# Norm and router arithmetic moved from GpSimd to VectorE, a bias moved into a matmul, FFN rounding moved into PSUM evictions, and new engine orders, in a two-layer fused kernel

## The chip, the cores and the metric

One Trainium2 chip, one of its cores. The metric is the device time of one execution in microseconds (us). The five engines are TensorE (PE; its weight loads are shown apart as PEld), VectorE (DVE), ScalarE (ACT), GpSimd (POOL) and SyncE (SP, which here only issues DMAs). Each has its own program and its own sequence of instructions; they meet through semaphores.

## The reference

Sixteen batches of 128 tokens by 128 features run through four residual stages:

```python
x = x + tanh(g_xattn[0]) * xattn0(ctx, ctx, layernorm(x))   # stage a: 16 heads, softmax over the HEADS
x = x + tanh(g_ffn[0])   * moe(layernorm(x))                # stage m: 8 experts, top 2, silu(x w0) * (x w1) -> wo
x = x + tanh(g_xattn[1]) * xattn1(layernorm(x), ctx)        # stage f: cat[c, c2q, c*c2q, c*q2c] @ W_l.T + b_l
x = x + tanh(g_ffn[1])   * bitffn(layernorm(x))             # stage g: 128 -> 512 gate/up -> 128

layernorm(x) = (x - mean(x)) / sqrt(var(x) + 1e-5)
moe:    w = softmax(top2(x @ gate)); sum over the 2 chosen experts of w * expert(x)
bitffn: each activation is scaled by 127/max|x| of its row and rounded to whole numbers
        ahead of each matmul; weights are rounded to -1, 0, 1 times their mean size
```

## The kernel before

The batches go through in eight pairs (256 tokens each). All four stages of a pair run on the one core, and neighbouring pairs overlap: while pair p is in the experts, pair p+1 is in attention and pair p-1 in the stages f and g. Weights stay in SBUF; SP loads them at the start. Matmuls of stages a and m are split into a high and a low part (`_hi`, `_lo`, three matmuls per product, `ps_z<-m_xhi,w_hi`, `m_xhi,w_lo`, `m_xlo,w_hi`).

**The order of the work.** Every engine's program is a list of steps, and two tables, `WHEN` (a step of each pair) and `ONCE` (a step of the start, and the spare matmuls `pe.warm_*`), give each step a number per pair; `order(engine)` sorts an engine's steps by these numbers. The tables thus set the order on each engine alone; waits between engines are semaphores.

**Stage a.** K and Q are projected, split into three bf16 parts (`qk_parts`), stored by SP to `rows_dram` and fetched as `k_rows` and `q_rows`. Four units per pair then go through `head_max` (DVE), `shifted` (DVE), `attn<-shifted` (ACT, the exponential), `tree` (POOL, four adds that sum over the heads), `head_inv` (DVE) and `attn<-attn,head_inv` (POOL). Then the weighted values, the output projection and x1.

**A layernorm** (a, m, f and g: four a pair, 32 in all) is `BN_STATS` and `BN_AGGR` on DVE (`*_mv`), four tiny instructions of 128x2 on POOL in `rstd` (add eps, negate the mean, raise to the power -1/2, multiply), and two ACT instructions that apply scale and bias.

**Stage m.** Sixteen up tiles: PE writes `ps_z`, ACT makes `m_tanh`, DVE `m_u`, and DVE or POOL `m_h` (POOL has seven of the sixteen). Eight `down` products go to `ps_d`; the first two experts' are added to `y` by ACT and POOL, the other six by DVE (`y<-ps_d,weights,y`). The router takes the difference of the top two logits (`tdiff`, DVE), its exponential (`texp`, ACT), five tiny POOL instructions for the two probabilities (`pool.top_probs`), and on DVE four instructions and a sum that make `weights`.

**Stage f** ends with four products into `late_bank` (`pe.f_z`) and, on DVE, x3 = th * product + `y_res`, where POOL has made `y_res` = `y` + bias (`pool.y_res`).

**Stage g** rounds by adding the constant `ROUND` (1.5 * 2^23) in f32 and taking it off again. The first activation: `g_r` (ACT, adds it), `g_q` (DVE, takes it off, to bf16), a PE transpose, `g_qt` (ACT copies out of PSUM). The second: `g_pr` (ACT, adds it), `g_pq` (ACT, takes it off, to bf16), four PE transposes for a batch, `g_pt` (ACT copies out of PSUM), the down product.

Each pair writes one `y`, so POOL's first add of a pair waits until the pair before has read it. `spare` issues PE matmuls on an identity (`ps_f<-ident_bf`) whose result nobody reads.

Of the kernel before, what the change touches and what calls it, by code (L numbers as in the profile page):

```python
# [13 lines left out]
P = 128  # L14
# [33 lines left out]
    "sp.load_a": (12, 1501, 2546, 3638, 7464, 12475, 17304, 20931),  # L48
    "sp.store_parts": (
# [6 lines left out]
    ),  # L56
    "sp.fetch_rows": (
        (1960, 3826, 7126, 11165, 15185, 19034, 23535, 27447),
        (2176, 3979, 7280, 10827, 14847, 18694, 23197, 27600),
    ),  # L60
    "sp.load_res": (2646, 5144, 9928, 12576, 16625, 22383, 25012, 28949),
    "sp.load_f": (2697, 11318, 15338, 19216, 24905, 27785, 31537, 34931),
    "sp.store": (16288, 20577, 24859, 28736, 32637, 36238, 38259, 39516),
    "pool.a_rstd": (467, 2292, 3414, 4828, 11299, 16757, 20361, 24484),
    "pool.ct_lo": (399, 2108, 2915, 8603, 12228, 13500, 20286, 21743),
    "pool.part3": (
        (1032, 2533, 6643, 10304, 14257, 18449, 22272, 26895),
        (1821, 3535, 7016, 10717, 14736, 18386, 23086, 27337),
    ),
    "pool.head_sum": (  # L70
# [4 lines left out]
    ),  # L75
    "pool.head_norm": (
# [14 lines left out]
    ),  # L91
    "pool.top_probs": (6705, 10149, 14319, 18585, 22334, 26625, 30788, 33972),
    "pool.y_res": (10367, 13574, 18312, 21817, 25821, 29981, 33448, 36784),
    "pool.f_rstd": (9408, 13378, 17534, 21621, 25895, 30055, 33522, 36662),
    "pool.f_prod": (11082, 15324, 19402, 23525, 27788, 31830, 34983, 37677),
    "pool.g_rstd": (12106, 15779, 20090, 24057, 28227, 32433, 35617, 38044),
    "pool.out": (16206, 20488, 24778, 28655, 32555, 36140, 38177, 0),
# [275 lines left out]
}  # L373

ONCE = {
    "sp.w_moe": 358,
    "sp.w_out": 113,
    "sp.w_fin": 1005,
    "sp.w_ffn": 853,
# [1435 lines left out]
```

## Time and profile before

| | |
|---|---|
| time, median of 3 runs | 398.3 us (397.81 to 398.43) |
| span of the profiled execution | 397.3 us |
| busy PE, PEld | 324.9, 284.0 us (82%, 71%) |
| busy DVE, POOL, ACT | 313.1, 299.1, 256.4 us (79%, 75%, 65%) |
| first `head_max` of pair 0, 1, 2, 3, 4, 7 | 28.2, 47.4, 81.4, 119.9, 159.4, 281.9 us |

The profile is of one execution; its span lies 1.0 us under the median. Busy times of the engines overlap, so none of them is the time. The first `head_max` of a pair marks where that pair's attention begins: from pair 3 to pair 7 the four pairs between are 162.0 us, 40.5 us each. The stretch before 28.2 us loads and splits weights; behind 320 us the last pair is alone.

### The profile page before, as it was taken

To read this page: it belongs to the slowest core of one execution; us is meant where nothing else is said; L and a number is where in the kernel's file an instruction comes from. 1 tells how busy PE (TensorE), PEld (TensorE's weight loads), DVE (VectorE), ACT (ScalarE), POOL (GpSimd) and SP (SyncE) were. 2 spreads that over 40 slices of the span, in tenths; PEclk is the share of its full clock that TensorE was granted. 3 is DMA by queue.
4 is the path that set the end of the run, shared out by engine and by line. 5 is a ranking of instruction groups with operands and counts; after the bars stand their busy time and mean duration, and the time that the engine had idled before them with its cause. 6 is when DMAs were issued, how large, how long until landed. Compare 5 with 4: busy or idle time off the path is not lost.

```text
span 397.3 us, 10407 instructions
## 1 busy us (share of the span) xinstructions
PE 324.9 (82%) x3326; PEld 284.0 (71%) x3326; DVE 313.1 (79%) x913; ACT 256.4 (65%) x726; POOL 299.1 (75%) x459
## 2 busy tenths in 40 slices
PE   1365589898999789979998899879978997996875
PEld 1255469787898679867986698669957896994742
DVE  2679877598869997999799979995989678778434
ACT  4335254536846797779667885777658855875754
POOL 4378989799898989898999799988778873443010
PEclk9999767999999999999999999998999999999585
DMA  5967210300341114012401221204100000000000
GB/s 161 289 192 210 81 36 21 116 17 16 88 115 34 29 41 128 19 56 63 108 15 47 68 87 29 61 6 131 33 16 1 28 15 2 2 29 14 2 13 13
DMA packets 34454, 24.17 MB, mean 61 GB/s; under 512 B 3617, under 2 KB 32097, under 8 KB 34401
## 3 DMA queue, kind: packets, MB, share of 16 engines
q1 hardware_dynamic: 33680, 23.32, 19.7%
q8 instruction: 27, 0.44, 0.5%
q10 hardware_dynamic: 720, 0.20, 0.2%
q14 instruction: 27, 0.21, 0.2%
HBM read 16.16 MB, written 7.34 MB: 59 GB/s over the span
## 4 chain that ended last, share of the span: by engine, by line
PE 37%; POOL 25%; DVE 13%; issue 10%; ACT 7%; DMA 4%; SPq 3%; POOLq 0%; DVEq 0%; ACTq 0%
POOL tree L939 9%; PE ps_d L1448 8%; POOL attn L945 8%; PE ps_z L1188 4%; PE ps_a L1196 3%; PE ps_z L1189 3%; PE ps_z L1190 3%; POOL m_h L876 2%; DVE head_max L1584 2%; DMA wf_raw<-in_wd 2%; DVE m_u L1623 1%; DMA k_rows<-rows_dram 1%; DVE y L1655 1%; PE ps_sc L1234 1%; DVE shifted L1590 1%
## 5 line engine op out<-in xcount | busy, mean ns | idle before, releaser
L1188 PE MATMUL ps_z<-m_xhi,w_hi 128*128 128x256 f32 x240 | 76.9, 320 | 12.7 <-DVE m_h L1631 6.1
L945 POOL TENSOR_TENSOR attn<-attn,head_inv 128x1024 f32<-128x1024 f32 x32 | 75.8, 2371 | 0.2 <-DVE head_inv L1606 0.2
L1448 PE MATMUL ps_d<-wdn,m_h 128*128 128x128 f32 x512 | 71.4, 283 | 4.7 <-DVE m_h L1631 2.1
L1448 PEld LDWEIGHTS ps_d<-wdn,m_h 128*128 128x128 f32 x512 | 63.1, 194 | 8.5 <-issue 4.1
L1189 PE MATMUL ps_z<-m_xhi,w_lo 128*128 128x256 f32 x240 | 68.8, 287 | 0.0
L1190 PE MATMUL ps_z<-m_xlo,w_hi 128*128 128x256 f32 x240 | 68.6, 286 | 0.0
L1623 DVE SCALAR_TENSOR_TENSOR m_u<-m_tanh,ps_z 128x256 f32<-128x256 f32 x120 | 49.0, 411 | 17.6 <-ACT m_tanh L1033 16.7
L1033 ACT ACTIVATE m_tanh<-ps_z 128x256 f32<-128x256 f32 x120 | 45.9, 384 | 26.0 <-PE ps_z L1190 25.6
L1188 PEld LDWEIGHTS ps_z<-m_xhi,w_hi 128*128 128x128 f32 x240 | 46.7, 195 | 19.3 <-issue 6.1
L876 POOL TENSOR_TENSOR m_h<-m_u,m_z 128x256 f32<-128x256 f32 x56 | 41.1, 734 | 17.2 <-DVE m_u L1623 17.2
L939 POOL TENSOR_TENSOR tree<-tree 128x256 f32<-128x256 f32 (+2 forms) x90 | 46.4, 515 | 7.1
L1189 PEld LDWEIGHTS ps_z<-m_xhi,w_lo 128*128 128x128 f32 x240 | 46.9, 196 | 0.0
L1190 PEld LDWEIGHTS ps_z<-m_xlo,w_hi 128*128 128x128 f32 x240 | 46.7, 195 | 0.0
L939 POOL TENSOR_TENSOR tree<-attn 128x512 f32<-128x512 f32 x30 | 38.3, 1277 | 6.5 <-ACT attn L1046 6.3
L1584 DVE TENSOR_REDUCE head_max<-ps_sc 128x64 f32<-128x1024 f32 x32 | 38.9, 1215 | 4.5 <-PE ps_sc L1234 4.2
L1046 ACT ACTIVATE attn<-shifted 128x1024 f32<-128x1024 f32 x32 | 33.7, 1055 | 10.1 <-DVE shifted L1590 10.1
L1590 DVE TENSOR_TENSOR shifted<-ps_sc,head_max 128x1024 f32<-128x1024 f32 x32 | 38.8, 1213 | 0.3
L1655 DVE SCALAR_TENSOR_TENSOR y<-ps_d,weights,y 128x128 f32<-128x128 f32 x96 | 28.8, 342 | 4.5 <-PE ps_d L1448 3.1
L1631 DVE TENSOR_TENSOR m_h<-m_u,ps_z 128x256 f32<-128x256 f32 x67 | 27.6, 414 | 5.8 <-PE ps_d L1448 5.1
L1031 ACT ACTIVATE m_z<-ps_z 128x256 f32<-128x256 f32 x53 | 20.2, 381 | 14.6 <-PE ps_z L1190 13.8
L1196 PE MATMUL ps_a<-attn,v_diag 128*32 128x128 f32 x512 | 20.4, 290 | 3.7 <-POOL attn L945 3.3
L1234 PE MATMUL ps_sc<-q_rows,k_rows 48*128 48x64 bf16 x512 | 13.7, 196 | 7.7 <-DVE shifted L1590 5.6
(311 smaller groups left out, 852.0 us busy)
## 6 DMA issues: line engine op xcount, KB each, us to landing
rows_dram<-qk_parts SPq DMA_DIRECT2D x16, 192.0 KB, 2.2
k_rows<-rows_dram SPq DMA_DIRECT2D x16, 192.0 KB
q_rows<-rows_dram SPq DMA_DIRECT2D x16, 192.0 KB
w_raw<-in_w SPq DMA_DIRECT2D x2, 1024.0 KB, 7.9
rows_dram<-qk_parts SPq DMA_DIRECT2D x16, 128.0 KB, 2.0
x_in<-in_x SPq DMA_DIRECT2D x8, 128.0 KB, 2.4
ct_in<-in_ctx_t SPq DMA_DIRECT2D x8, 128.0 KB, 2.4
rows_dram<-qk_parts SPq DMA_DIRECT2D x16, 64.0 KB, 1.7
```

The costliest lines, as they stand in the source:

```text
L876: pool.tensor_tensor(m_h[:, k % 4], m_u[:, k % 4], m_z1[:, n % 3], ALU.mult).then_inc(s_mhp, 1)
L939: pool.tensor_tensor(dst, src[:, 0:n, :], src[:, n:2 * n, :], ALU.add).then_inc(s_tree, 1)
L945: pool.tensor_tensor(e, e, head_inv[:, u % 2].unsqueeze(1).to_broadcast([P, HEADS, HALF]), ALU.mult).then_inc(s_attn, 1)
L1033: act.activation(m_tanh[:, k % 2], tile_bank(p, k)[:, 0:TOK], ACT.Tanh, scale=0.5).then_inc(s_mt, 1)
L1046: act.activation(attn[:, b, :, k0:k0 + HALF], shifted[:, u % 2], ACT.Exp).then_inc(s_exp, 1)
L1188: pe.matmul(dst, hi_w, hi_x, start=start, stop=False)
L1189: pe.matmul(dst, lo_w, hi_x, start=False, stop=False)
L1190: return pe.matmul(dst, hi_w, lo_x, start=False, stop=True)
L1448: last = pe.matmul(ps_d[:, b * P:(b + 1) * P], m_h[:, m % 4, b * P:(b + 1) * P], wdn[:, m], start=(k == 0), stop=(k == TPE - 1))
L1584: dve.tensor_reduce(head_max[:, u % 2], sc.rearrange("p h k -> p k h"), AX.X, ALU.max).then_inc(s_hmax, 1)
L1590: dve.tensor_tensor(shifted[:, u % 2], sc, head_max[:, u % 2].unsqueeze(1).to_broadcast([P, HEADS, HALF]), ALU.subtract).then_inc(s_shift, 1)
L1623: dve.scalar_tensor_tensor(m_u[:, k % 4], m_tanh[:, k % 2], 1.0, z[:, 0:TOK], ALU.add, ALU.mult).then_inc(s_mu, 1)
```

## The change

- `rstd` on POOL keeps only the power. The eps add (`add_eps`) and the product with the negated mean (`minus_mean_rstd`) become two DVE steps for each norm, each with a place of its own in DVE's order. ACT's norm waits for the second.
- The router's five POOL instructions become four on DVE (`dve.top_probs`, with a reciprocal in place of the power). The four that made `w_first` and `w_second` become two over both batches and both places (`top_eq`, `top_w`).
- `pool.y_res` goes. The bias of stage f is a third plane of `bias_parts` and is added by PE, one more matmul of `first_products` for each batch; x3 reads `y` itself. `y` has two buffers.
- Stage g: PE transposes the f32 values `g_r` and `g_pr`, and `ROUND` is taken off as the result leaves PSUM: `g_qt` (now on DVE) and `g_pt` (ACT). `g_q` (DVE), `g_qt` on ACT and `g_pq` (ACT) go.
- The third-stage bias is loaded as 96x128 with the stage a biases, not as 128x128. Three constants of the start go.
- All numbers of `WHEN` and `ONCE` are new.

```diff
-    "sp.load_a": (12, 1501, 2546, 3638, 7464, 12475, 17304, 20931),
+    "sp.load_a": (1, 658, 1926, 4484, 8345, 12225, 15475, 18558),
...
-            def rstd(p, s_mv, s_rs, mv, rs):
-
-                pool.wait_ge(s_mv, p.count(2, 2))
-                pool.tensor_tensor(rs[:, 0], mv[:, :, 1], eps_col[:], ALU.add).then_inc(s_rs, 1)
-                pool.tensor_tensor(rs[:, 1], mv[:, :, 0], minus_ones[:], ALU.mult).then_inc(s_rs, 1)
-                pool.wait_ge(s_rs, p.count(4, 1))
-                pool.tensor_tensor(rs[:, 2], rs[:, 0], minus_half[:], ALU.pow).then_inc(s_rs, 1)
-                pool.wait_ge(s_rs, p.count(4, 3))
-                pool.tensor_tensor(rs[:, 3], rs[:, 2], rs[:, 1], ALU.mult).then_inc(s_rs, 1)
+            def rstd(p, s_rs, s_norm, rs):
+
+                pool.wait_ge(s_rs, p.count(3, 1))
+                wait(pool, s_norm, p.before().count(2, 2))
+                pool.tensor_tensor(rs[:, 0], rs[:, 2], minus_half[:], ALU.pow).then_inc(s_rs, 1)
...
+            def add_eps(p, mv, rs, s_mv, s_rs):
+
+                dve.wait_ge(s_mv, p.count(2, 2))
+                dve.tensor_scalar(rs[:, 2], mv[:, :, 1], EPS, None, ALU.add).then_inc(s_rs, 1)
+
+            def minus_mean_rstd(p, mv, rs, s_rs):
+
+                dve.wait_ge(s_rs, p.count(3, 2))
+                dve.scalar_tensor_tensor(rs[:, 1], mv[:, :, 0], -1.0, rs[:, 0], ALU.mult, ALU.mult).then_inc(s_rs, 1)
...
-                if p := due(now, "pool.top_probs"):
-
-                    pool.wait_ge(s_texp, p.count(1, 1))
...
+                if p := due(now, "dve.top_probs", 0):
+
+                    dve.wait_ge(s_texp, p.count(1, 1))
+                    dve.tensor_scalar(tsum[:], texp[:], 1.0, None, ALU.add).then_inc(s_tp, 1)
+                if p := due(now, "dve.top_probs", 1):
+                    dve.wait_ge(s_tp, p.count(4, 1))
+                    dve.reciprocal(tinv[:], tsum[:]).then_inc(s_tp, 1)
+                if p := due(now, "dve.top_probs", 2):
+                    dve.wait_ge(s_tp, p.count(4, 2))
...
+                    dve.tensor_scalar(tprob[:, :, 0:1], tinv[:], th_half[:, 0:1], None, ALU.mult).then_inc(s_tp, 1)
+                    dve.scalar_tensor_tensor(tprob[:, :, 1:2], texp[:], th_half[:, 0:1], tinv[:], ALU.mult,
+                                             ALU.mult).then_inc(s_tp, 1)
...
-                    for b in range(2):
-                        for k, dst in enumerate((w_first, w_second)):
-                            dve.tensor_scalar(dst[:, b], expert_no[:], top_nof[:, b, k:k + 1],
-                                              tprob[:, b, k:k + 1], ALU.is_equal, ALU.mult).then_inc(s_w12, 1)
+                    dve.wait_ge(s_tp, p.count(4, 4))
+                    dve.wait_ge(s_teq, p.count(1, 1))
+                    dve.tensor_tensor(top_w[:], top_eq[:], tprob[:].unsqueeze(3).to_broadcast([P, 2, 2, EXPERTS]),
+                                      ALU.mult).then_inc(s_w12, 1)
...
-                if p := due(now, "pool.y_res"):
...
-                    pool.tensor_tensor(y_res[:], y[:], bl_all[:].unsqueeze(1).to_broadcast([P, 2, P]),
-                                       ALU.add).then_inc(s_fyb, 1)
...
+            def first_products(p, b):
+
+                s = slice(b * P, (b + 1) * P)
+                pe.matmul(late_bank(p, b)[:, s], ones_bf[:], bias_parts[:, 2], start=True, stop=False)
+                pe.matmul(late_bank(p, b)[:, s], f_ct[:, s], wl[:, 0], start=False, stop=False)
...
-                    if p := due(now, "act.g_pq", b):
-
-                        act.wait_ge(s_gpr, p.count(2, b + 1))
-                        wait(act, s_gpt, p.before().count(2, 2))
-                        act.activation(g_pq[:, b], g_pr[:, b], ACT.Copy, bias=-ROUND).then_inc(s_gpq, 1)
...
-                        act.activation(g_pt[:, b], batch_bank(p, b)[:, 0:TOK].bitcast(BF16), ACT.Copy).then_inc(s_gpts, 1)
+                        act.activation(g_pt[:, b], batch_bank(p, b)[:], ACT.Copy, bias=-ROUND).then_inc(s_gpts, 1)
...
-                            pe.transpose(batch_bank(p, b)[:, k * HALF:(k + 1) * HALF].bitcast(BF16),
-                                                g_pq[:, b, k * P:(k + 1) * P], ident_bf[:])
+                            pe.transpose(batch_bank(p, b)[:, k * P:(k + 1) * P],
+                                                g_pr[:, b, k * P:(k + 1) * P], ident[:])
...
-                if p := due(now, "dve.g_q"):
-                    wait(dve, s_gqt, p.before().count(1, 1))
...
+                if p := due(now, "dve.g_qt"):
+                    wait(dve, s_gu, p.before().count(4, 4))
...
+                        dve.tensor_scalar(g_qt[:, cols(g)], batch_bank(p, g[0])[:, cols(g)], ROUND, 127.0, ALU.subtract,
+                                          ALU.min).then_inc(s_gqs, 1)
```

Where the tables put things is read from the order of the built programs. First SP at the start. `w_raw` are the expert weights w0 and w1 (1 MB each), `wf_raw` the three FFN weights, `gains`, `bias_raw` and `wo_t` belong to stage a's output, `wcq` and `bsum` to stage f; before, from the first load of `x_in` and `ct_in` on:

```order
L756 DMA gains<-in_g_xattn 128x2
...
L760 DMA wo_t<-in_wo 128x128
L750 DMA w_raw<-in_w 128x8x256
...
L770 DMA wf_raw<-in_wd 128x4x128
L763 DMA wcq<-in_w_cq 128x1
...
L766 DMA bl_all<-in_bl 128x128
L791 DMA rows_dram<-qk_parts 128x3x256 [waits s_k1]
```

and after:

```order
L755 DMA w_raw<-in_w 128x8x256
...
L774 DMA wf_raw<-in_wd 128x4x128
L761 DMA gains<-in_g_xattn 128x2
...
L765 DMA wo_t<-in_wo 128x128
L783 DMA x_in<-in_x 128x2x128 [waits s_axn]
L785 DMA ct_in<-in_ctx_t 128x2x128 [waits s_ctlo]
L795 DMA rows_dram<-qk_parts 128x3x256 [waits s_k1]
```

The bulk loads now lead, the seven small loads of `wcq`, `bsum` and `bl_all` no longer stand ahead of the first store of `qk_parts` (six of them follow the fetches of `q_rows`), and the next pair's two loads do.

Second, POOL in a middle pair, at a norm. Before, that of stage g, with `m_h` ahead of it and `attn` behind:

```order
L876 TENSOR_TENSOR m_h<-m_u,m_z 128x256
L843 TENSOR_TENSOR g_rs<-g_mv,eps_col 128x2
L844 TENSOR_TENSOR g_rs<-g_mv,minus_ones 128x2
L846 TENSOR_TENSOR g_rs<-g_rs,minus_half 128x2
L848 TENSOR_TENSOR g_rs<-g_rs 128x2
L945 TENSOR_TENSOR attn<-attn,head_inv 128x16x64
```

and after, those of stages m and f:

```order
L873 TENSOR_TENSOR m_h<-m_u,m_z 128x256
L845 TENSOR_TENSOR m_rs<-m_rs,minus_half 128x2
L920 TENSOR_TENSOR attn<-attn,head_inv 128x16x64
L892 TENSOR_TENSOR o_sb<-o_raw,x 128x256
L845 TENSOR_TENSOR f_rs<-f_rs,minus_half 128x2
```

A norm is now one POOL instruction of 128x2 where there were four. What DVE holds between the two tiny instructions of stage m's norm, L1465 (eps) and L1470 (the product), in a middle pair after the change:

```order
L1465 TENSOR_SCALAR m_rs<-m_mv 128x2
L1615 SCALAR_TENSOR_TENSOR m_u<-m_tanh,ps_z 128x256
L1752 RECIPROCAL g_sc<-g_amc 128x2
L1753 SCALAR_TENSOR_TENSOR g_sc<-g_amc,cg 128x2
L1615 SCALAR_TENSOR_TENSOR m_u<-m_tanh,ps_z 128x256
L1623 TENSOR_TENSOR m_h<-m_u,ps_z 128x256 x2
L1647 SCALAR_TENSOR_TENSOR y<-ps_d,weights,y 128x128 x2
L1470 SCALAR_TENSOR_TENSOR m_rs<-m_mv,m_rs 128x2
L1576 TENSOR_REDUCE head_max<-ps_sc 128x64
```

Eight of DVE's instructions lie between the two, and the next unit's `head_max` stands right behind the one that waits for POOL.

Third, PE between the value projection of pair 1 (`ps_a<-ct_hi,wqkv_hi`) and pair 0's gate, before:

```order
L1188 MATMUL ps_a<-ct_hi,wqkv_hi 128x256
L1189 MATMUL ps_a<-ct_hi,wqkv_lo 128x256
L1190 MATMUL ps_a<-ct_lo,wqkv_hi 128x256
L1243 MATMUL ps_d<-ident,m_xn 128x128 x2
L1213 MATMUL ps_f<-ident_bf 128x128 x8
L1234 MATMUL ps_sc<-q_rows,k_rows 128x64 x16
```

and after:

```order
L1152 MATMUL ps_a<-ct_hi,wqkv_hi 128x256
L1153 MATMUL ps_a<-ct_hi,wqkv_lo 128x256
L1154 MATMUL ps_a<-ct_lo,wqkv_hi 128x256
L1184 MATMUL ps_f<-ident_bf 128x128 x32
L1233 MATMUL ps_a<-ident,a_xn 128x128 x2
L1214 MATMUL ps_d<-ident,m_xn 128x128 x2
L1184 MATMUL ps_f<-ident_bf 128x128 x12
L1205 MATMUL ps_sc<-q_rows,k_rows 128x64 x16
```

Where eight spare matmuls (`ps_f`) stood, there are 44.

## Rows read from the trace of the kernel before

**Rows 1.** Windows of the span; us, then busy time (instructions) by engine, clock, DMA.

```profile
28.15:119.90 91.75, 75.50 (x899) 67.78 (x899) 73.39 (x173) 47.16 (x125) 83.06 (x112) 0.91 0.27 81
119.90:281.90 162.00, 143.68 (x1540) 127.47 (x1538) 142.69 (x431) 120.72 (x351) 144.65 (x222) 0.99 0.20 58
320.00:397.30 77.30, 62.59 (x475) 51.59 (x473) 50.22 (x180) 49.47 (x146) 24.48 (x50) 0.87 0.04 12
```

**Rows 2.** POOL timeline at 158 us: start, length, engine, line, operation, tiles.

```profile
158.44 0.20 POOL L843 TENSOR_TENSOR g_rs<-g_mv,eps_col 128x2 f32<-128x2 f32 x1
...
158.74 0.70 POOL L846 TENSOR_TENSOR g_rs<-g_rs,minus_half 128x2 f32<-128x2 f32 x1
...
159.66 2.38 POOL L945 TENSOR_TENSOR attn<-attn,head_inv 128x1024 f32<-128x1024 f32 x1
```

**Rows 3.** POOL timeline at 144 us, the router.

```profile
144.66 0.21 POOL L885 TENSOR_TENSOR tsum<-texp,ones 128x2 f32<-128x2 f32 x1
...
146.16 0.73 POOL L876 TENSOR_TENSOR m_h<-m_u,m_z 128x256 f32<-128x256 f32 x1
```

**Rows 4.** Instructions by line, POOL, 28 to 320 us: count, busy, mean ns, idle before.

```profile
L889 POOL TENSOR_TENSOR tsum<-tsum,minus_one 128x2 f32<-128x2 f32 x7 | 4.9, 700 | 0.5
L846 POOL TENSOR_TENSOR m_rs<-m_rs,minus_half 128x2 f32<-128x2 f32 x7 | 4.9, 699 | 0.0
...
L912 POOL TENSOR_TENSOR y_res<-y,bl_all 128x256 f32<-128x256 f32 x6 | 4.4, 731 | 0.0
L846 POOL TENSOR_TENSOR f_rs<-f_rs,minus_half 128x2 f32<-128x2 f32 x6 | 4.2, 700 | 0.0
L846 POOL TENSOR_TENSOR a_rs<-a_rs,minus_half 128x2 f32<-128x2 f32 x6 | 4.2, 694 | 0.0
L846 POOL TENSOR_TENSOR g_rs<-g_rs,minus_half 128x2 f32<-128x2 f32 x5 | 3.5, 701 | 0.0
```

**Rows 5.** Waits of POOL, 28 to 320 us: who, for whom, us, times, longest.

```profile
POOL tree L939 <- ACT attn L1046: 6.3, 8, 1.3
...
POOL qk_parts L869 <- ACT qk_parts L1022: 3.6, 2, 2.2
POOL tsum L885 <- ACT texp L1079: 1.6, 3, 0.9
```

**Rows 6.** Instructions by line, ACT: count, busy us, mean ns, idle before.

```profile
L1172 ACT ACTIVATE g_pq<-g_pr 128x512 bf16<-128x512 f32 x16 | 10.0, 627 | 0.0
```

**Rows 7.** SP timeline, the first 24 us (issues, not landings).

```profile
4.13 0.43 SPq L750 DMA_DIRECT2D w_raw<-in_w  x1
...
5.23 3.38 SPq L754 DMA_DIRECT2D gate_raw<-in_gate  x1
...
10.08 1.20 SPq L763 DMA_DIRECT2D wcq<-in_w_cq  x1
...
14.17 1.50 SPq L791 DMA_DIRECT2D rows_dram<-qk_parts  x3
```

**Rows 8.** DVE timeline at the start.

```profile
16.23 1.75 DVE L1542 TENSOR_REDUCE wabs<-wf_raw 128x3 f32<-128x1536 f32 x1 [3.22 <-DMA wf_raw<-in_wd]
...
28.15 1.23 DVE L1584 TENSOR_REDUCE head_max<-ps_sc 128x64 f32<-128x1024 f32 x1 [0.52 <-PE ps_sc L1234]
```

**Rows 9.** Window with the clock at half, 55.1 to 65.3 us.

```profile
55.10:65.30 10.20, 9.67 (x60) 8.80 (x61) 8.86 (x21) 5.29 (x12) 9.73 (x12) 0.50 0.11 33
```

**Rows 10.** Chain that ended last, 390 to 395 us: start, length, what.

```profile
392.29 0.62 ACT g_pq L1172
```

**Rows 11.** Two DVE lines with two SBUF inputs: ns min/median/max.

```profile
L1669 DVE TENSOR_TENSOR weights<-w_first,w_second x8: 163/174/260, 71.8 to 343.0; 128x16 f32<-128x16 f32 x8
...
L1642 DVE TENSOR_TENSOR tdiff<-top x8: 144/330/657, 64.5 to 339.1; 128x2 f32<-128x2 f32 x8
```

**Rows 12.** DVE timeline at 146 us, and the same line in the page, part 5.

```profile
146.24 0.74 DVE L1623 SCALAR_TENSOR_TENSOR m_u<-m_tanh,ps_z 128x256 f32<-128x256 f32 x2
...
L1623 DVE SCALAR_TENSOR_TENSOR m_u<-m_tanh,ps_z 128x256 f32<-128x256 f32 x120 | 49.0, 411 | 17.6 <-ACT m_tanh L1033 16.7
```

More of the change, by code:

```diff
@@ L92 @@
[L92 to L97, printed above, removed]
[7 rows of a table added]
+    ),
+    "pool.f_prod": (9223, 12965, 16563, 20126, 23964, 27864, 30805, 33218),
@@ L373 @@
+    "dve.top_probs": (
[3 rows of a table added]
+    ),
+    "dve.top_eq": (5196, 8762, 12397, 15981, 19303, 23401, 26825, 30376),
+    "dve.g_qt": (10808, 14746, 18452, 21713, 25584, 28985, 31976, 33985),
 }
 ONCE = {
[L376 to L379, printed above, removed]
-    "sp.w_late": 2804,
-    "act.qkv_hi": (717, 371, 697),
-    "act.w_hi": (1899, 1476, 4321, 1804),
-    "act.gate_hi": 2328,
-    "act.th": 851,
-    "pool.w_lo": (1588, 2685),
-    "pe.w_total": 1735,
-    "dve.qkv_scale": (382, 1305),
@@ new lines @@
+    "act.th": 1095,
+    "pool.w_lo": (1429, 1837),
+    "pe.w_total": 1181,
+    "dve.qkv_scale": (599, 781),
+    "dve.qkv_lo": (705, 685, 1521),
+    "dve.w_lo": (4625, 5783),
+    "dve.gate_lo": 4282,
+    "dve.w_small": 4576,
+    "dve.w_abs": 1003,
+    "dve.w_scale": 1582,
+    "dve.w_round": (1637, 1703, 2044),
+    "dve.w_clip": (3123, 3730),
+    "dve.bias_parts": 1169,
+    "act.wo_scale": 3230,
+    "pe.warm_f": (32220, 32242, 32509, 32531, 32552, 32797, 32818, 32840, 32862, 32994, 33016, 33217, 34064, 34086),
@@ L602, in build @@
         f_w4 = sb("f_w4", [P, 2, P])
-        y_res = sb("y_res", [P, 2, P])
         x3s = sb("x3", [P, 2, 2, P])
@@ L614, in build @@
         g_r = sb("g_r", [P, 2, P])
-        g_q = sb("g_q", [P, 2, P], BF16)
         g_qt = sb("g_qt", [P, TOK], BF16)
@@ L1077, in _ @@
                     act.wait_ge(s_tdf, p.count(1, 1))
-                    wait(act, s_tp, p.before().count(5, 5))
+                    wait(act, s_tp, p.before().count(4, 4))
                     act.activation(texp[:], tdiff[:], ACT.Exp).then_inc(s_texp, 1)
@@ L1140, in _ @@
                     act.wait_ge(s_gsc, p.count(3, 3))
-                    wait(act, s_gq, p.before().count(1, 1))
+                    wait(act, s_gqt, p.before().count(1, 1))
                     for b in range(2):
@@ L1147, in _ @@
                     act.activation(g_sc[:, :, 1], g_amc[:], ACT.Identity, scale=cg[:, 0:1]).then_inc(s_gsz, 1)
-                if p := due(now, "act.g_qt"):
-                    wait(act, s_gu, p.before().count(4, 4))
-                    for g in groups(p):
-                        act.wait_ge(s_gqt, p.count(1, 1) + g[0])
-                        act.activation(g_qt[:, cols(g)], batch_bank(p, g[0])[:, g[0] * HALF:(g[-1] + 1) * HALF].bitcast(BF16),
-                                       ACT.Copy).then_inc(s_gqs, 1)
                 for u in range(4):
@@ L1163, in _ @@
                         act.wait_ge(s_gps, p.count(4, 2 * b + 2))
-                        wait(act, s_gpq, p.before().count(2, b + 1))
+                        wait(act, s_gpt, p.before().count(2, b + 1))
                         act.activation(g_pr[:, b], g_p[:, b], ACT.Identity, scale=g_ps[:, b, 0:1],
@@ L1486, in stats @@
             def stats(p, x, st, mv, s_st, s_mv, s_rs):
-                wait(dve, s_rs, p.before().count(4, 4))
+                wait(dve, s_rs, p.before().count(3, 3))
                 for b in range(2):
@@ L1643, in _ @@
                     dve.wait_ge(s_topi, p.count(2, 2))
-                    wait(dve, s_w12, p.before().count(4, 4))
+                    wait(dve, s_teq, p.before().count(1, 1))
                     dve.tensor_copy(top_nof[:], top_no[:]).then_inc(s_tnof, 1)
@@ L1668, in _ @@
                     wait(dve, s_y, p.before().count(2 * DVE_SUMS, 2 * DVE_SUMS))
-                    dve.tensor_tensor(weights[:], w_first[:], w_second[:], ALU.add).then_inc(s_w, 1)
+                    dve.tensor_tensor(weights[:], top_w[:, :, 0], top_w[:, :, 1], ALU.add).then_inc(s_w, 1)
                 if p := due(now, "dve.a_xlo"):
```

399 lines of the change are left out of this document (197 added, 202 removed), and 271 rows, old and new, of the table WHEN.

## The prediction

> **What bounds the kernel now.** I read the windows first, because shares over the whole span mix four different stretches. From the first `head_max` to pair 3's, 91.75 us, POOL is busy for 83.06 us, more than PE (75.50) or DVE (73.39). In the middle, four pairs in 162.00 us, three engines stand close together: POOL 144.65, PE 143.68, DVE 142.69, each about 89%. Behind 320 us the last pair is alone and POOL has 24.48 of 77.30 us: there a chain of latencies sets the end [rows 1]. So up to 320 us I take POOL as the engine on which the others wait, by a narrow margin in the middle.
>
> Then POOL's timeline, to see what it does between the large instructions. A norm begins at 158.44, its power starts at 158.74 and the next large instruction at 159.66: 1.22 us for four instructions that work on two numbers a row, with the power .77 (158.74 to 159.51) of it [rows 2]. The five router instructions hold POOL from 144.66 to 146.16, 1.50 us [rows 3]. Last, POOL's waits between 28 and 320 us. The largest that ACT causes are 6.3 us ahead of `tree`, 3.6 ahead of `qk_parts`, 1.6 ahead of the router's first instruction [rows 5]. So POOL is not wholly a wall: some of its idle time is ACT being late.
>
> At the start POOL is no limit: SP is. The store of `qk_parts` is issued at 14.17, behind a row of small loads from 10.08 on and behind `gate_raw`, whose issue took 3.38 us [rows 7]. DVE waits 3.22 us for `wf_raw` and then spends 1.75 on its absolute sums; the first `head_max` comes at 28.15 [rows 8].
>
> **The change part by part, against the span of 397.3 us.**
>
> *Tiny work off POOL.* Between 28 and 320 us the power has 24 rows (m 7, f 6, a 6, g 5), the router 7, `y_res` 6 at .73 us [rows 4]. A norm keeps its power: 1.22 − .77 = .45 saved. 24 × .45 = 10.8; 7 × 1.5 = 10.5; 6 × .73 = 4.4; together 25.7 us. Where POOL is the engine waited for, the end moves by all of it: **−25.7**. That is at once the largest term and the most doubtful, since in the middle the other engines have only 1 to 2 us less work than POOL. The lower bound of the gain is what the next engine allows, below under the rivals.
>
> *What DVE gets.* A pair has 14 new tiny instructions (8 for norms, 4 for probabilities, 2 for weights). The nearest row is the sum of the weights, 163 ns at least and 174 in the median [rows 11]: at most 14 × .174 = 2.4 us a pair, if each cost its whole row. They don't quite: two `m_u` in a row fill .74 us where their line has a mean of 411 ns [rows 12], so rows overlap at their ends. And four instructions for the router's weights and `g_q` go. I take the net at nothing on the path, because DVE's own idle time covers it (162.00 − 142.69 = 19.3 us over four pairs, 4.8 a pair) [rows 1]; the other end is the whole 2.4 a pair.
>
> *What PE gets.* Four f32 transposes in place of bf16 ones for a batch, and one more product of 128 columns for each. PE stands idle 18 us of the 162 [rows 1]; nothing on the path, and in the last pair a few tenths, which I take against the saved rows there.
>
> *ACT.* `g_pq` goes: 16 of 627 ns, 10.0 us [rows 6], and the copy for `g_qt` goes to DVE. ACT is no bound anywhere, but POOL waits for it. The wait ahead of the router's POOL work (1.6) goes with that work; of the 9.9 us ahead of `tree` and `qk_parts` [rows 5] I take a little under half, 4.4, because ACT is late there for DVE and PE as well. **−6**, bounds 0 and −11.5.
>
> *The start.* In the new order the two 1 MB loads and `wf_raw` lead, then six small loads, and the store of `qk_parts` no longer stands behind the seven loads from 10.08 to 14.17 (4.1 us) [rows 7]. SP is then free for it at about 11.5 by its own rows, 2.7 us sooner, and it issues the stores for q without a pause between them and k. DVE's 3.22 us wait for `wf_raw` [rows 8] shrinks, since that load is issued sooner. The two together, 2.7 + 3.2, are 5.9: **−6** for the first `head_max` (28.15 to about 22). Bounds: −2, if the gains and `wo_t`, now issued behind 2.75 MB of bulk, land late and hold DVE and ACT, which read them ahead of the first scores; −9, if the wait of 3.22 and the 1.75 of the absolute sums, the store and the fetch all draw together.
>
> *The clock in pair 0.* From 55.10 to 65.30 us the granted clock is .50, that is the 1.2 GHz level, with PE busy 9.67 of 10.20 us [rows 9]. So the first up tiles run at half clock. The changed order has 44 spare matmuls ahead of that stretch where there were 8. If the clock rises earlier, the most that can be won is half of PE's 9.67, 4.8 us; **−2**, bounds 0 and −4.8.
>
> *Two y buffers.* POOL's first add of a pair no longer waits for the pair before. None of POOL's larger waits is that one, so it is worth nothing by itself; it lets the add stand where POOL has time.
>
> *The tail.* On the chain that ended last, `g_pq` stands at 392.29 with .62 us [rows 10]. Each of the last pair's two batches goes through it, and through `g_q`, once; the two batches lie partly side by side. The norms there cross between engines once more (POOL's power, then DVE's product, then ACT) and lose three POOL rows of .15 to .20 [rows 2]. I take **−2** in all; bounds 0 and −6, the latter with a higher clock in the tail, where the mean is .87 [rows 1].
>
> Sum: 397.3 − 25.7 − 6 − 6 − 2 − 2 = 355.6 of span. The median lies 1.0 us above this span, so 356.6: **357 us**.
>
> **A rule weighed against the trace.** The two rows that DVE has with two small inputs from SBUF: the sum of weights takes 163 to 260 ns, the difference of the top two 144 to 657 with a median of 330, while POOL is busy nine tenths of the time [rows 1, 11]. So a DVE instruction of this kind lost at most .5 us here, and never the 2.38 us of an `attn` [rows 2].
> The Trainium skill, "SBUF — State Buffer", section "Who interferes with whom", says that a DVE instruction with two SBUF inputs contends with a GpSimd instruction that reads SBUF, since they share a read interface, and that whichever comes second is blocked. By that rule taken fully, the change would move work from GpSimd into the very form that GpSimd blocks; the rows just named do not bear out so large a price.
>
> **The rivals.**
>
> *DVE becomes the bound.* For: in the middle DVE has only 2 us less than POOL. With 4 × 2.4 = 9.6 us more it has 142.7 + 9.6 = 152.3 in that stretch, more than POOL's 144.65 − 4 × (4 × .45 + 1.5 + .73) = 128.5. If it then fills its time almost wholly, the stretch shrinks from 162 to about 153 in place of 146, and the pairs before lose 1 or 2 us too: 366 us. Against: the rows' overlap, the instructions removed. If DVE kept the idle share that it has now, the time would end near 375.
>
> *The norms wait on DVE.* DVE stands in its order at the product of mean and power until POOL has done the power. Behind it in the example stands `head_max`, on which the whole next unit of attention waits; ahead of POOL's power can stand an `attn` of 2.38 or a `tree`. For: POOL's place for the power is fixed by its order, and a pair has four such places. Against: eight DVE instructions stand between eps and product in that example, some 3 us at about .4 each, the mean of `m_u` [rows 12]. At .5 us a norm, 32 × .5 = 16: 373 us.
>
> *Shared access between DVE and POOL.* This is the rival on the other side. Seven of a pair's added instructions have two SBUF inputs (four products for norms, one probability, two for weights), 56 in all. If each blocked DVE, or POOL, for half an `attn`, 1.19 us, that were 66 us: 423 us. It turns a gain into a loss from 41/56 = .74 us each on. The largest row of the kind is .66 [rows 11], which includes its own work; so I give it little.
>
> *All of it comes through.* ACT's relief in full (5.5 more), the clock in full (2.8 more), a start of −8: 346 to 350 us.
>
> *The change does not act.* POOL's wins could be swallowed by new waits at other places, with only the start and the tail left: 397.3 − 8 + 1, about 390; to come out within .2% of before, which is .8 us and about what a measurement of this kernel can tell from none, the start would have to fail as well.
>
> **How the numbers follow.** Forecast (351 to 363) .57; DVE bound .15; norm waits .12; all of it .10; shared access .03; no effect or something else .03. The range that leaves out no more than two in ten reaches from the best case, 346, to beyond the norm waits at 373 and DVE bound with its idle share at 375: 346 to 376. Slower: the shared access and a small part of the rest, .035; same .015; faster .95.
>
> **What would show it.** Right: the first `head_max` at about 22 us; four pairs in the middle in about 146 us in place of 162; POOL's busy time there near 128; rows of .15 to .2 us for the new DVE lines; no idle time of DVE at the products of the norms above .3 us a norm; a clock above .5 where pair 0's up tiles start; no `g_pq` in the chain. Wrong: the pairs in the middle still 40 us apart with DVE over 95% busy (DVE is the bound), or with DVE waiting for POOL at the products (the norms), or rows of over .7 us in the new DVE lines (shared access); a first `head_max` later than 26 us would say that the loads, not SP's order, set the start.

## The result and the profile after

The changed kernel takes 414.5 us (median of 4 runs, 412.86 to 416.73) beside 398.06 us (397.55 to 398.43) before: 1.0408 times as long, 95% interval 1.0364 to 1.0452. The forecast was 357 us and faster; the kernel is slower and lies outside the range of 346 to 376. Some executions of a kernel take longer at a lower mean granted clock: the medians in this document are of all executions, while the ratios leave those out, so what a run wins or loses is told by the ratios.

The page of the changed kernel, its span and the busy time of each engine:

```profile
span 414.9 us, 10337 instructions
...
PE 333.1 (80%) x3342; PEld 292.1 (70%) x3342; DVE 352.2 (85%) x992; ACT 249.1 (60%) x701; POOL 266.8 (64%) x312
```

POOL has lost 32 us of work (299.1 before), as was meant. DVE has gained 39 (313.1 before) with 79 instructions more, which is .5 us for each, though most of the new ones work on two numbers a row. The same windows as in [rows 1], cut at the first `head_max` of pair 0, 3 and 7 (columns as there), and a late stretch at half clock:

```profile
27.10:126.20 99.10, 73.57 (x893) 65.46 (x891) 89.46 (x194) 48.95 (x128) 79.94 (x85) 0.90 0.27 80
126.20:290.00 163.80, 142.77 (x1523) 127.72 (x1514) 158.42 (x456) 114.56 (x333) 126.47 (x148) 0.98 0.19 57
306.60:323.60 17.00, 14.90 (x104) 12.78 (x104) 12.28 (x38) 6.33 (x16) 7.95 (x10) 0.50 0.06 17
```

Pairs 0 to 2 take 99.10 us where they took 91.75, and DVE is busy for 90% of it, not 80%. The four pairs of the middle take 163.80 (162.00 before) with DVE at 158.42, or 97%, and POOL down from 144.65 to 126.47. From pair 7's first `head_max` to the end there are 124.9 us where there were 115.4. With 1.1 us won at the start, −1.1 + 7.4 + 1.8 + 9.5 is the 17.6 us between the two spans (16.4 between the medians).

Which rows most of DVE's 39 us are, the lines of the changed kernel say (count, busy us, mean ns, idle before):

```profile
L1470 DVE SCALAR_TENSOR_TENSOR m_rs<-m_mv,m_rs 128x2 f32<-128x2 f32 x8 | 8.7, 1083 | 0.0
L1470 DVE SCALAR_TENSOR_TENSOR f_rs<-f_mv,f_rs 128x2 f32<-128x2 f32 x8 | 7.5, 939 | 0.4 <-POOL f_rs L845 0.4
...
L1465 DVE TENSOR_SCALAR a_rs<-a_mv 128x2 f32<-128x2 f32 x8 | 6.1, 759 | 0.1
L1470 DVE SCALAR_TENSOR_TENSOR g_rs<-g_mv,g_rs 128x2 f32<-128x2 f32 x8 | 4.6, 572 | 1.6 <-POOL g_rs L845 1.6
...
L1658 DVE TENSOR_SCALAR tsum<-texp 128x2 f32<-128x2 f32 x8 | 3.6, 456 | 0.6 <-ACT texp L1054 0.6
...
L1752 DVE RECIPROCAL g_sc<-g_amc 128x2 f32<-128x2 f32 x8 | 1.3, 156 | 0.1
```

A product of two numbers a row takes 1083 ns on average in stage m, while a reciprocal of the same size takes 156. The idle time ahead of these rows is small: they don't wait for a semaphore, they are long. The timeline at one of them, first DVE, then POOL:

```profile
303.10 0.16 DVE L1752 RECIPROCAL g_sc<-g_amc 128x2 f32<-128x2 f32 x1
303.17 0.20 DVE L1753 SCALAR_TENSOR_TENSOR g_sc<-g_amc,cg 128x2 f32<-128x2 f32 x1
303.31 2.30 DVE L1470 SCALAR_TENSOR_TENSOR m_rs<-m_mv,m_rs 128x2 f32<-128x2 f32 x1
305.54 0.41 DVE L1615 SCALAR_TENSOR_TENSOR m_u<-m_tanh,ps_z 128x256 f32<-128x256 f32 x1
```

```profile
302.57 0.70 POOL L845 TENSOR_TENSOR m_rs<-m_rs,minus_half 128x2 f32<-128x2 f32 x1
303.24 2.36 POOL L920 TENSOR_TENSOR attn<-attn,head_inv 128x1024 f32<-128x1024 f32 x1
305.55 1.28 POOL L914 TENSOR_TENSOR tree<-attn 128x512 f32<-128x512 f32 x1
```

POOL ends the power and begins `attn` at 303.24. DVE comes to the product at 303.31, .07 us later, and its row ends at 305.61, within .02 us of `attn`'s end at 305.60. Behind it stands the next `m_u`; over the whole run POOL waits 32.4 us for `m_u`, where it waited 17.2 before. So DVE comes to the product when the power is done, and meets what POOL's order has right behind the power; in this place that is an `attn`.

It is not this row alone. Of the 64 norm rows on DVE, 25 take over 350 ns, and by the timelines each of the 25 ends 13 to 24 ns behind the end of a POOL instruction that had begun before it.

The row at 303.31 reaches PE too. Behind it in DVE's order stands `g_qt`, for which PE waits; first both, then windows of the 3.4 us ahead of the row and the 3.4 us from there on (columns as in [rows 1]):

```profile
307.05 0.41 DVE L1759 TENSOR_SCALAR g_qt<-ps_g 128x256 bf16<-128x256 f32 x1
307.51 0.61 PE L1354 MATMUL ps_g<-wf_q,g_qt 128*128 128x256 bf16 x2 [2.50 <-DVE g_qt L1759]
299.75:303.17 3.42, 3.15 (x29) 3.14 (x30) 3.42 (x16) 2.71 (x6) 1.51 (x3) 1.00 0.01 2
303.17:306.60 3.43, 1.78 (x28) 1.33 (x26) 3.43 (x8) 2.35 (x7) 3.43 (x3) 0.99 0.00 0
```

PE's busy time falls from 3.15 to 1.78 us, and at 306.60 begins the stretch of 17 us at .50, the 1.2 GHz level, shown above. That the one brought on the other is read from their order; no run shows it.

### The profile page after: what moved, and what is told of

It is laid out like the page before. It is cut to its first block and busy times, and to the rows that moved or that the text cites. A ratio compares the mean times of both kernels' runs of the same rounds, so it can differ in the third digit from the quotient of the medians.

```text
span 414.9 us, 10337 instructions
## 1 busy us (share of the span) xinstructions
PE 333.1 (80%) x3342; PEld 292.1 (70%) x3342; DVE 352.2 (85%) x992; ACT 249.1 (60%) x701; POOL 266.8 (64%) x312
## 5 line engine op out<-in xcount | busy, mean ns | idle before, releaser
L873 POOL TENSOR_TENSOR m_h<-m_u,m_z 128x256 f32<-128x256 f32 x56 | 41.1, 734 | 32.6 <-DVE m_u L1615 32.4
L1152 PEld LDWEIGHTS ps_z<-m_xhi,w_hi 128*128 128x128 f32 x240 | 46.9, 196 | 17.2 <-issue 8.1
L1205 PE MATMUL ps_sc<-q_rows,k_rows 48*128 48x64 bf16 x512 | 14.0, 198 | 16.2 <-DMA q_rows<-rows_dram 8.4
L1205 PEld LDWEIGHTS ps_sc<-q_rows,k_rows 48*128 48x128 bf16 x512 | 10.2, 99 | 20.8 <-issue 10.5
```

The lines of the kernel that those rows point to most:

```text
L873: pool.tensor_tensor(m_h[:, k % 4], m_u[:, k % 4], m_z1[:, n % 3], ALU.mult).then_inc(s_mhp, 1)
L1152: pe.matmul(dst, hi_w, hi_x, start=start, stop=False)
```

## The experiments

Theory S, shared access: a tiny DVE instruction with two inputs from SBUF, or a `TENSOR_SCALAR` of an even row of f32, can't run while POOL reads SBUF, and stands until POOL's instruction ends. Theory O, the rival: the new orders and the crossings between the engines cost the time. The times below are medians, beside runs of the kernel before on the same chip (398.6 to 399.9 us); ratios carry their 95% interval.

**The norms in another form.** The same work on DVE, at the same places, in instructions of 128x1 that take the power as a per-row scalar:

```diff
-                dve.tensor_scalar(rs[:, 2], mv[:, :, 1], EPS, None, ALU.add).then_inc(s_rs, 1)
+                for b in range(2):
+                    dve.tensor_scalar(rs[:, 2, b:b + 1], mv[:, b, 1:2], EPS, None, ALU.add).then_inc(s_rs, 1)
...
-                dve.scalar_tensor_tensor(rs[:, 1], mv[:, :, 0], -1.0, rs[:, 0], ALU.mult, ALU.mult).then_inc(s_rs, 1)
+                for b in range(2):
+                    dve.tensor_scalar(rs[:, 1, b:b + 1], mv[:, b, 0:1], rs[:, 0, b:b + 1], -1.0, ALU.mult,
+                                      ALU.mult).then_inc(s_rs, 1)
```

> The changed kernel with its norms in another form on VectorE: the eps add as two instructions of 128x1, the product with the mean as two of 128x1 that take the power as a per-row scalar, so no instruction of a norm has two SBUF tensors or an even row of f32. Orders unchanged, 64 more instructions on VectorE. Theory S (VectorE's tiny instructions stand until a GpSimd instruction that shares their access to SBUF ends): all eps and product rows .14 to .20 us, VectorE's busy time down by about 20 us, time about 400 us (396 to 406). Theory O (the new orders and the crossings between the engines cost the time, the rows only show it): rows or waits move, time 412 to 418 us.

Measured: 400.58 us (394.83 to 406.7), .9989 of before (.995 to 1.0028). Its lines for the norms:

```profile
L1472 DVE TENSOR_SCALAR g_rs<-g_mv,g_rs 128x1 f32<-128x1 f32 x16 | 2.6, 207 | 1.6 <-POOL g_rs L845 1.6
...
L1472 DVE TENSOR_SCALAR m_rs<-m_mv,m_rs 128x1 f32<-128x1 f32 x16 | 2.5, 195 | 0.0
...
L1466 DVE TENSOR_SCALAR a_rs<-a_mv 128x1 f32<-128x1 f32 x16 | 1.7, 146 | 0.1
```

Twice the instructions, and 17 us of rows where there were 33: none of the 128 is over 215 ns. By the ratios the time falls by 4.2% of the kernel before, about 17 us, with every order as it was. Theory S as expected, but for a detail: the products take .2 us, not .15.

**The norms back on POOL, in the new orders.** POOL's four instructions stand where the changed kernel has the power; DVE's two steps go:

```diff
+                pool.tensor_tensor(rs[:, 2], mv[:, :, 1], eps_col[:], ALU.add).then_inc(s_rs, 1)
+                pool.tensor_tensor(rs[:, 3], mv[:, :, 0], minus_ones[:], ALU.mult).then_inc(s_rs, 1)
...
-                    minus_mean_rstd(p, m_mv, m_rs, s_mrs)
```

> The changed kernel with the norms' four tiny instructions back on GpSimd, at the place of the power; the router, the bias, the rounding and all orders stay as changed. Theory S: VectorE loses 64 rows that took 33 us, GpSimd gains 32 x .45 = 14 us in which it has room, time 398 to 405 us. Theory O: places stay, GpSimd has more to do, time 412 to 422 us.

Measured: 395.6 us, .9912 (.9882 to .9941): faster than both kernels, than the one before by .9%. POOL has 14 us more to do than in the changed kernel, and the end comes about 20 us sooner. Theory S, and 2 us below its range.

**The router in small forms too.** As the first run, with the router's DVE steps in 128x1 and the expert weights as four instructions of 128x8 with per-row scalars:

```diff
-                    dve.tensor_scalar(tsum[:], texp[:], 1.0, None, ALU.add).then_inc(s_tp, 1)
+                    for b in range(2):
+                        dve.tensor_scalar(tsum[:, b], texp[:, b], 1.0, None, ALU.add).then_inc(s_tp, 1)
...
-                    dve.tensor_tensor(top_w[:], top_eq[:], tprob[:].unsqueeze(3).to_broadcast([P, 2, 2, EXPERTS]),
-                                      ALU.mult).then_inc(s_w12, 1)
+                            dve.tensor_scalar(top_w[:, b, j], expert_no[:], top_nof[:, b, j:j + 1],
+                                              tprob[:, b, j:j + 1], ALU.is_equal, ALU.mult).then_inc(s_w12, 1)
```

> As e1, and the router's tiny instructions on VectorE likewise in 128x1 or per-row-scalar form, the expert weights as four instructions with per-row scalars as in the kernel before; only their sum keeps two SBUF tensors. Theory S: about 8 us of stretched rows more than in e1 go, of which some are paid back by 7 more instructions a pair: 1 to 6 us below e1, about 396 us. Theory O: not below e1, 412 to 420 us.

Measured: 409.03 us, 1.0169 (1.0079 to 1.026). A miss: by the ratios about 7 us above the first run. The line that came instead:

```profile
L1677 DVE TENSOR_SCALAR top_w<-expert_no,top_nof,tprob 128x8 f32<-128x8 f32 x32 | 13.5, 488 | 0.1
```

I had taken this form as safe, since in the kernel before it took about 290 ns. Here its mean is 488: four rows of 128x8 in place of two of 128x32, and they stretch. The rows of 128x1 did come down (`tsum` to 144). Of the 32, 13 are over 350 ns, and each ends 25 to 29 ns behind the end of a POOL instruction. An odd row isn't safe either: the cast of `top_nof`, 128x3 here, has three rows of .55 to 2.15 us that end beside POOL's in the same way. What theory S had wrong is which forms are safe, not what happens.

**The changed arithmetic in the old orders.** Each new step stands at the place of the step it replaces:

```diff
-    "dve.a_nmr": (448, 1513, 4290, 6835, 9744, 13950, 17838, 21403),
+    'dve.a_nmr': (567, 2392, 3514, 4928, 11399, 16857, 20461, 24584),
```

> The changed kernel's arithmetic in the orders of the kernel before: every step that both have at its old place, the eps add right behind the statistics, the product 1 us of the table behind the power, the router's steps where GpSimd had them, the eviction with the rounding where ScalarE's copy stood. Theory S: the tiny instructions stand behind GpSimd here too, time 400 to 415 us. Theory O: without the new orders the removed work counts, time 375 to 392 us.

Measured: 442.97 us, 1.1075 (1.1014 to 1.1137), far above both theories' bounds. The norms' product in stage m has a mean of 1124 ns here. To part the access from the crossing, the same with the norms in 128x1 form (edit as in the first run):

> The changed arithmetic in the old orders, with the norms on VectorE in 128x1 form. Theory S alone: most of what those orders lose to the norms' rows goes, 415 to 428 us. If what they lose is the crossing (GpSimd standing for eps, VectorE for the power), the time stays at 435 us or more.

Measured: 425.34 us, 1.0644 (1.0594 to 1.0695). By the ratios, 17 of the 43 us went with the form of the norms, that is with their access to SBUF. The other 26 are neither that nor the new orders; POOL waits 38.0 us for `m_u` and 26.1 ahead of `tree` in this run (17.2 and 6.3 before). The rest of the change in the same orders takes 401.35 us (below), so they belong to the norms and the router on DVE. That the crossings of the norms make them is likely, but was not taken apart.

**The old arithmetic in the new orders.** The kernel before with the changed kernel's tables:

```diff
-    "sp.load_a": (12, 1501, 2546, 3638, 7464, 12475, 17304, 20931),
+    'sp.load_a': (1, 658, 1926, 4484, 8345, 12225, 15475, 18558),
```

> The kernel before, with all its arithmetic (norms and router on GpSimd, y_res, the rounding on ScalarE and VectorE), in the new orders; its own steps stand where their successors stand (the router's probabilities where VectorE has its first of them, y_res behind the last product added to y). Theory S (the shared access is what costs the time, the orders are sound): 390 to 402 us, near the kernel before. Theory O (the new orders cost it): 412 us or more.

Measured: 418.91 us, 1.0472 (1.0385 to 1.0559): a miss for theory S, and as theory O had it. The change's arithmetic alone (443 us) is slower than both together (414.5), and its orders alone (419) are no faster, so the loss isn't the rows' alone. Part of it is the access again: `w_first`, 303 ns in the kernel before, has a mean of 647 here, and nine of its 16 rows end with a POOL instruction, where two did before. The rest was not taken apart.

**Norms and router back on POOL, in the new orders.**

```diff
+                    pool.tensor_tensor(tsum[:], tsum[:], minus_one[:].unsqueeze(1).to_broadcast([P, 2, 1]),
+                                       ALU.pow).then_inc(s_tp, 1)
...
-                    dve.reciprocal(tinv[:], tsum[:]).then_inc(s_tp, 1)
```

> As the run with the norms back on GpSimd, and the router's five instructions back on GpSimd too with the four per-row-scalar instructions for the expert weights on VectorE. What is left of the change: no y_res and two y buffers, the bias on TensorE, the rounding in the evictions, the orders. Theory S: the 10 to 13 us of stretched router rows go, GpSimd gets 12 us in which it has room: 386 to 393 us. Theory O: the same as with the norms alone, 394 to 400 us.

Measured: 408.87 us, 1.0263 (1.0217 to 1.031). A miss for both theories: 13 us above the run with the norms alone on POOL. The run changes two things, the engine of the probabilities and the form of the weights. The weights in the old form stretch as in the third run (571 ns, 16.2 us, where the two instructions in their place take 5.9 with the norms alone on POOL), so it doesn't show on which engine the router is better.

**The disputed cost by itself.** The kernel before, with 32 instructions more on DVE that wait for nobody and that nobody reads, first a product of two SBUF constants:

```diff
+                        dve.scalar_tensor_tensor(idle[:, 4 * p.c + u], minus_ones[:], -1.0, minus_half[:], ALU.mult, ALU.mult)
```

> The kernel before with 32 idle instructions more on VectorE: at the place where a norm's product would stand, -1 times one constant times another, 128x2, both from SBUF, read by nobody and waiting for nobody. It measures the disputed cost by itself. Theory S: mean row .5 to .7 us instead of .15, VectorE's busy time 16 to 22 us up, time 6 to 14 us over before. Theory O (no cost but the waits between engines, of which there are none here): rows of .15 us, time within 3 us of before.

then a reciprocal of one constant at the same places:

```diff
+                        dve.reciprocal(idle[:, 4 * p.c + u], minus_half[:])
```

> As the run with idle products, at the same 32 places a reciprocal of one 128x2 constant in place of the product: one SBUF input, the form whose rows never stretched. Theory S: rows of .16 us, VectorE 5 us up, time within 3 us of before. Theory O: the same as the run with idle products.

Their lines, of the products and of the reciprocals:

```profile
L1572 DVE SCALAR_TENSOR_TENSOR idle<-minus_ones,minus_half 128x2 f32<-128x2 f32 x32 | 20.9, 654 | 0.0
```

```profile
L1572 DVE RECIPROCAL idle<-minus_half 128x2 f32<-128x2 f32 x32 | 4.9, 152 | 0.0
```

Measured: with the products a median of 427.32 us (420.65 to 428.27), with the reciprocals 399.42 us, 1.0015 (.9993 to 1.0037). The lowest time with the products is 21.6 us over the median of the kernel before (399.05), and that is what I count: thirty-two products of two numbers a row cost 22 us or more, as many reciprocals nothing. Eleven of the products are over 350 ns, and each ends 16 to 19 ns behind the end of a POOL instruction; half of the 32 take 154 ns or less, as the reciprocals do (160 at most). So a product isn't long by itself. This shows what theory S says on a kernel without the new orders and without crossings. The cost is above the 6 to 14 us that S expected: the rows' 20.9 us came through whole, where the expectation left a part of them to DVE's idle time.

**The rest of the change in the old orders.** No `y_res`, two `y`, the bias on PE, the rounding in the evictions; norms and router as before:

```diff
-                    pool.tensor_tensor(y_res[:], y[:], bl_all[:].unsqueeze(1).to_broadcast([P, 2, P]),
-                                       ALU.add).then_inc(s_fyb, 1)
...
-                        act.activation(g_pq[:, b], g_pr[:, b], ACT.Copy, bias=-ROUND).then_inc(s_gpq, 1)
```

> The parts of the change that put nothing tiny on VectorE (no y_res, two y buffers, the bias on TensorE, the rounding in the evictions), in the orders of the kernel before; norms and router on GpSimd as before. By the prediction's own prices 4.4 us of y_res, some of ScalarE's 13 us and a little of the tail come: 388 to 396 us. Theory S has nothing against it. Theory O: the old orders are good, so the same. If it is no faster than before, GpSimd's work is not what the end waits for.

Measured: 401.35 us, 1.0051 (1.0026 to 1.0076): a miss, a little slower than before. In these orders these parts alone win nothing.

**Tiny POOL work left out, nothing added.** The kernel before, so that the largest term of the sum stands alone:

```diff
-                pool.tensor_tensor(rs[:, 0], mv[:, :, 1], eps_col[:], ALU.add).then_inc(s_rs, 1)
-                pool.tensor_tensor(rs[:, 1], mv[:, :, 0], minus_ones[:], ALU.mult).then_inc(s_rs, 1)
...
-                pool.tensor_tensor(rs[:, 3], rs[:, 2], rs[:, 1], ALU.mult).then_inc(s_rs, 1)
+                pool.tensor_tensor(rs[:, 2], mv[:, :, 1], minus_half[:], ALU.pow).then_inc(s_rs, 1)
```

> The kernel before with tiny GpSimd work left out and nothing put in its place: a norm keeps the power alone (of the bare variance, the bias a constant), the router two of its five instructions (its probabilities are not the reference's). 24 x .45 + 7 x 1.1 = 18.5 us less on GpSimd between 28 and 320 us. If GpSimd is what the end waits for, as the prediction has it: 376 to 384 us. If its idle work is covered (the rival that the run without y_res points to): 392 to 399 us.

Measured: 395.27 us, .9875 (.9813 to .9936): by the ratio about 5 us (2.6 to 7.5) for 18.5 us of work, the rival's answer. What took its place, POOL's waits between 28 and 320 us (columns as in [rows 5]):

```profile
POOL tree L927 <- ACT attn L1034: 14.7, 13, 2.3
POOL m_h L871 <- DVE m_u L1611: 13.2, 8, 3.2
POOL qk_parts L864 <- ACT qk_parts L1010: 5.8, 2, 3.3
```

POOL waits 8.4 us more for ACT's exponential than in [rows 5], 2.2 more ahead of `qk_parts`, and 13.2 us for `m_u` (6.0 before in the same stretch). So most of its work had been covered: it was busy, not waited for.

**The new orders without tiny DVE work.** The changed kernel without DVE's norm steps and probabilities:

```diff
-                if p := due(now, "dve.m_nmr"):
-                    minus_mean_rstd(p, m_mv, m_rs, s_mrs)
...
-                    dve.tensor_scalar(tsum[:], texp[:], 1.0, None, ALU.add).then_inc(s_tp, 1)
```

> The changed kernel without its tiny VectorE work: a norm is the power alone (of the bare variance, the bias a constant), and the router's four probability instructions are left out with a constant in their place; the two for the weights stay. Orders as changed. If the shared access and the added rows are all that stands between the change and the forecast: 352 to 370 us. If the removed GpSimd work is worth little anyway: 378 to 390 us.

Measured: 391.79 us, .9826 (.9751 to .99), 2 us above the second answer. With the 64 norm rows and the four of the probabilities gone the change wins 7 us, not 41. The router's other rows stay and still stretch (`tdiff` 522 ns, `weights` 416, `top_eq` 376, `top_w` 365), so this isn't the whole of the new cost.

**A version for use.** The norms on POOL, the router's difference, sum and probabilities in 128x1 on DVE, the rest as changed (edits as in the second and third run, without the 128x8):

> The run with the norms back on GpSimd in the new orders, and of the router's steps on VectorE the difference, the sum and the two probabilities as instructions of 128x1 with per-row scalars (24 more instructions in all, none of 128x8). Theory S: 9.8 us of stretched rows go, 4 us of rows come: 388 to 395 us. Theory O: no faster than without, 395 to 400 us.

Measured: 395.86 us, .9941 (.9908 to .9974). Faster than both kernels, than the one before by .6%, but no better than the run with the norms on POOL alone, as theory O had it. That one stays the best here of the versions that can be used.

## Why the prediction was wrong, by its own steps

**What DVE gets: the step that set the sign.** "I take the net at nothing on the path", 174 ns a row from the sum of weights, 2.4 us a pair at most. The norms' rows alone took 33.1 us, or 4.1 a pair, DVE's busy time rose by 39 us, 4.9 a pair, and by the ratios 17 us of the time went with the form of the norms and 20 with their return to POOL. So DVE's idle time did not cover the new rows, and their count was not what made them dear: each row's length was. In size it is the smaller part of the miss, as far as a run shows it: of the 57 us between 357 and 414.5, 23 lie above the run without the tiny DVE work (391.8), and the other 35 between that run and the forecast are terms of the sum that did not come.

**The weighing of the rule: how that came about.** I wrote that these rows lost at most .5 us "while POOL is busy nine tenths of the time". That is an average over the stretch, not what POOL did at these rows. Here is one of the eight sums, at 188.54 on DVE, and POOL around it in the kernel before:

```profile
188.54 0.16 DVE L1669 TENSOR_TENSOR weights<-w_first,w_second 128x16 f32<-128x16 f32 x1
```

```profile
187.19 0.20 POOL L894 TENSOR_TENSOR tprob<-texp,tsum 128x2 f32<-128x2 f32 x1
188.70 0.73 POOL L876 TENSOR_TENSOR m_h<-m_u,m_z 128x256 f32<-128x256 f32 x1 [1.31 <-DVE m_u L1623]
```

POOL stood idle from 187.39 to 188.70 us. In the old order the sum follows POOL's own router work, and there POOL waits for DVE: 163 ns is here the length of a row with no POOL instruction beside it. The median of `tdiff`, 330 ns [rows 11], was the sign: it is a row of .14 us whose median instance is stretched, and the three of its eight that are over 350 ns each end 13 to 17 ns behind a POOL instruction, in the kernel before already. The Trainium skill, "SBUF — State Buffer", section "Who interferes with whom", says that a DVE instruction with two SBUF inputs contends with a GpSimd instruction that reads SBUF and that the later one is blocked; the trace after agrees (2.30 us beside an `attn` of 2.36), and the products and reciprocals in the kernel before agree (654 against 152 ns). The same section names `tensor_scalar` among the operations that can enter a mode with both ports and so contend, when their operands meet its conditions; the eps rows of stage a, 759 ns at 128x2 and 146 at 128x1, agree with that. The rival "shared access" had the mechanism, at a chance of .03. Its price of 1.19 us a row was too high (the products' mean was .71, of which .55 is lost), and its count too low, since the eps adds and `tsum` belong to it.

**Tiny work off POOL, −25.7: wrong by itself.** The condition stood in the text ("where POOL is the engine waited for"), and I took it as met because POOL had the longest busy time. Leaving out 18.5 us of it won about 5. POOL, PE and DVE lay within 2 us of each other in the middle [rows 1]; with less of POOL's work its waits for ACT and DVE grew by 17.8 us in that run (8.4, 2.2 and 7.2).

**ACT, −6.** ACT did lose 7 us of busy time (256.4 to 249.1), but the run that holds this relief, with `y_res` gone too, is .5% slower than before.

**The start, −6: −1.1.** SP's issues in the changed kernel:

```profile
2.88 3.62 SPq L759 DMA_DIRECT2D gate_raw<-in_gate  x1
...
8.30 1.56 SPq L761 DMA_DIRECT2D gains<-in_g_xattn  x1
...
13.68 3.42 SPq L795 DMA_DIRECT2D rows_dram<-qk_parts  x6
...
20.34 1.35 SPq L803 DMA_DIRECT2D q_rows<-rows_dram  x2
```

The store comes at 13.68 (14.17 in [rows 7]), not at 11.5: `gate_raw` still takes 3.6 us to issue, and the small loads from `gains` on, which stand behind it now, 4.4. The stores of k and q do go out without a pause, as said, and both fetches are issued 1.2 us sooner (q rows at 20.34, 21.54 before; k rows at 18.79, 19.98 before); `head_max` starts at 27.05 (28.15 in [rows 8]). The sign "later than 26 us" thus came true: the order of SP's issues was worth 1.2 us, not 2.7. DVE's wait ahead of the absolute sums did not go either: its order now has the next pair's statistics ahead of them, and there it waits 6.77 us for `x_in`.

**The clock, −2, and the tail, −2.** The sign for the clock came true: pair 0's first up tile starts at 66.6 us, and the clock is 1.00 from 54.0 on. But the stretch at half moved ahead of it, 33.5 to 54.0, and is longer: 20.5 us, where the kernel before has 6.8 and 10.2 (the latter in [rows 9]). In the whole run 58 us are at half, 41 before, and the mean granted clock is .930 (.948 before). So the term itself has the wrong sign. The 17 us at 306.60 fall in the last pair, where the kernel before ran at full:

```profile
281.90:320.00 38.10, 33.33 (x354) 28.99 (x353) 32.75 (x95) 28.32 (x82) 32.84 (x47) 1.00 0.05 15
```

From pair 7's first `head_max` to the end it is 9.5 us longer, where the forecast had the tail 2 shorter. How much of that is the clock and how much the stretched rows was not taken apart. No `g_pq` is on the chain any more, as said.

**Rivals.** DVE as the bound: DVE has 97% of the middle, as that rival said, with 158.42 us where it counted 152.3: by stretched rows and not by their number. Norms that wait: DVE's waits for the power are 2.9 us in all (1.6, .9 and .4 by stage), so DVE seldom stands at the product for the power. It is the other way round: POOL waits for the eps adds, 18.3 us in stage f and 9.9 in stage g over the whole run, where it waited 4.4 and 5.4 for the statistics before.

**Still open.** Why the new orders lose with the old arithmetic (419 us) and the old ones with the new (443), and what sets the 392 us that are left when most of DVE's tiny work is gone. Putting the statistics into PSUM, to give DVE a source outside SBUF, was not tried.

## What to carry to other kernels

Moving tiny work from GpSimd to VectorE can cost more than it frees: price the moved row by what GpSimd does at that instant, not by the shortest row of its kind, and prefer forms that stayed short here (128x1 with a per-row scalar, a reciprocal). An engine with the longest busy time is not yet the one that the end waits for: leave its work out in one run, add nothing, and see whether the end moves. A median row that is twice the shortest of its form can be a wait that the idle columns don't show: compare its end with the ends of the other engine's rows.

## What was unexpected in the hardware

A wait of this kind has no idle time ahead of it: it is inside the row's own duration, so it counts as busy time, and DVE looked 85% busy. Thirty-two products of two numbers a row cost 22 us or more on a kernel of 399, which is all of the 20.9 us of their rows. The same add of stage a takes 759 ns on average as one instruction of 128x2, and 146 as 128x1, in the same orders. The rows that stretch end within 30 ns of the end of a POOL instruction, which is how they are told from rows that are long by themselves.
